# An attention and expert block on one core: which step of a gap takes a bank of the bursts, and goes first

## The reference

```
h = layernorm(x) * (1 + ca) + sa
x = x + ga * attention(h)          # 16 heads of 16, softmax over 1024 keys, projection
h = layernorm(x) * (1 + cb) + sb
x = x + gb * ffn(h)                # one base matrix, and the adapter of 8 that rebuilds h best
```

## Time and profile before

| | us |
|---|---|
| median of 3 runs | 1008.89 |
| the 3 runs | 1008.31, 1010.95, 1008.89 |
| span of the profiled execution, first to last instruction | 1004.2 |
| PE busy, share of the span | 962.7, 96% |
| DVE busy | 813.2, 81% |
| ACT busy | 661.7, 66% |
| granted TensorE clock, mean over the span | 0.988 |

### The profile page before, as it was taken

How to read it: one execution, slowest core, us unless ns; L and a number is a source line. 1 busy time by engine, 2 the same in 40 slices (tenths; PEclk the granted TensorE clock), 3 DMA queues, 4 the chain that set the end, 5 groups by cost and what they waited for, 6 DMA issues and landing times.

```text
span 1004.2 us, 16485 instructions
## 1 busy us (share of the span) xinstructions
PE 962.7 (96%) x5794; PEld 480.8 (48%) x5794; DVE 813.2 (81%) x1657; ACT 661.7 (66%) x1295; POOL 284.4 (28%) x391
## 2 busy tenths in 40 slices
PE   6989999999899999999999999999999999999998
PEld 5444344343344445554454454545454455644476
DVE  4789989899688887788888888788778788889455
ACT  2148787887577777667668786766657767666831
POOL 4210133022155241200336431300237413116320
PEclk9879999999899999999999999999999999999999
DMA  6850051242550513242223511404424311132001
GB/s 180 141 92 23 12 107 45 56 95 71 80 96 12 96 34 66 44 85 81 70 87 60 85 44 45 75 13 78 130 70 80 58 29 35 38 96 77 29 6 48
DMA packets 47890, 66.93 MB, mean 67 GB/s; under 512 B 12139, under 2 KB 32112, under 8 KB 47796
## 3 DMA queue, kind: packets, MB, share of 16 engines
q1 hardware_dynamic: 46572, 65.00, 29.9%
q0 software_dynamic: 384, 0.79, 0.5%
q10 hardware_dynamic: 852, 0.09, 0.1%
HBM read 27.48 MB, written 12.59 MB: 40 GB/s over the span
## 4 chain that ended last, share of the span: by engine, by line
PE 77%; DVE 9%; ACT 5%; issue 2%; POOL 2%; DMA 2%; SPq 1%; ACTq 0%; DVEq 0%; POOLq 0%
PE pE L811 25%; PE pO L811 22%; PE pX L811 18%; PE pM L811 11%; DVE mx L1293 4%; ACT P L1118 2%; DMA QO<-lo 1%; ACT h1T L1159 1%; DVE h2f L1454 1%; ACT h2f L1205 1%; ACT hi L1175 1%; DVE lo L1374 1%; SPq L1867 0%; DVE junk L1430 0%; DMA P<-in_wmod 0%
## 5 line engine op out<-in xcount | busy, mean ns | idle before, releaser
L1293 DVE TENSOR_REDUCE mx<-pM 128x1 f32<-128x512 f32 x1006 | 629.7, 682 | 76.7 <-PE pM L811 71.4
L1118 ACT ACTIVATE P<-pE 128x512 f32<-128x512 f32 x996 | 526.7, 601 | 181.1 <-PE pE L811 177.8
L811 PE MATMUL pM<-KO,QO 48*128 48x512 f32 x1006 | 370.7, 455 | 6.8 <-DMA QO<-lo 3.3
L811 PE MATMUL pE<-QO,KO 50*128 50x512 f32 x996 | 349.2, 438 | 11.9 <-ACT h1T L1159 5.1
L811 PEld LDWEIGHTS pE<-QO,KO 50*128 50x128 f32 x996 | 164.9, 187 | 234.1 <-issue 125.1
L811 PE MATMUL pO<-P,V 128*17 128x512 f32 x2048 | 257.9, 598 | 5.1 <-ACT P L1118 5.1
L811 PEld LDWEIGHTS pM<-KO,QO 48*128 48x128 f32 x1006 | 164.3, 187 | 41.3 <-DVE mx L1293 28.8
L811 PEld LDWEIGHTS pO<-P,V 128*17 128x17 f32 x2048 | 40.5, 96 | 103.2 <-issue 88.1
L1695 POOL CAST mh<-mxc 128x16 fp32r<-128x16 f32 x32 | 6.5, 203 | 285.7 <-DVE mxc L1302 285.5
L811 PE MATMUL pX<-h1T,wqkv_s 128*128 128x512 f32 x112 | 59.2, 642 | 1.9 <-DVE lo L1374 1.5
L1754 POOL TENSOR_TENSOR Hs<-h2f,Hs 128x512 fp32r<-128x512 f32 x28 | 35.7, 1284 | 83.6 <-ACT Hs L1235 68.3
(11 more groups left out here) (301 smaller groups left out, 1023.4 us busy)
## 6 DMA issues: line engine op xcount, KB each, us to landing
outs<-osb SPq DMA_DIRECT2D x31, 256.0 KB, 2.9
KO<-hi SPq DMA_DIRECT2D x56, 128.0 KB, 4.0
QO<-hi SPq DMA_DIRECT2D x56, 128.0 KB, 5.1
x<-in_x SPq DMA_DIRECT2D x20, 256.0 KB, 3.6
out<-x SPq DMA_DIRECT2D x16, 256.0 KB, 2.1
AT<-outs SPq DMA_DIRECT2D x15, 256.0 KB
asum<-wsum SPq DMA_DIRECT2D x15, 256.0 KB
KO<-lo SPq DMA_DIRECT2D x28, 128.0 KB, 3.6
```

The costliest lines, as they stand in the source:

```text
L811: return e.matmul(o, lhsT, rhs, start=start, stop=stop)
L1118: e.activation(P[:, u % 3, j, :], bank(s), ACT.Exp).then_inc(*empties(s))
L1293: e.tensor_reduce(mx[:, hq % 2, k:k + 1, kh], bank(s), AX.X, ALU.max, negate=True).then_inc(*empties(s))
```

## The change

A new function `arrange` goes over the finished list, gap by gap, between the first and the last E. In a gap it looks at the banked steps. One of them "stays": the one whose pieces are already open in the side bank, or else one left open by this gap, or else the last. The others are "ahead" if each is whole within the gap, is of another kind than the one that stays, and needs nothing of the same gap. Then their pieces go to the head of the gap, ahead of the copies, the quiet steps, P V and the step that stays, and they take a bank of the bursts (0 to 5). If one of them does not qualify, the gap is left alone. Nothing is added to or taken from the work.

```diff
--- before.py
+++ after.py
@@ -471,11 +471,41 @@
     return out
 
 
+def arrange(out):
+
+    first = next(n for n, s in enumerate(out) if s[0] == "E")
+    stop = max(n for n, s in enumerate(out) if s[0] == "E")
+    made, ahead, held, gap = list(out[:first]), set(), None, []
+    for s in out[first:stop + 1]:
+        if s[0] not in ("E", "M", "mmax"):
+            gap.append(s)
+            continue
+        if gap:
+            seen = [x if isinstance(x[0], tuple) else (x, 0) for x in gap]
+            here = list(dict.fromkeys(x for x, _ in seen if x[0] in BANKED))
+            ends = [x for x in here if (x, PIECES.get(x[0], 1) - 1) in seen]
+            open_ = [x for x in here if x not in ends]
+            stays = held or (open_ or here or [None])[-1]
+            front = [x for x in here if x != stays and x in ends and (x, 0) in seen and (not stays or x[0] != stays[0])
+                     and not any(d == y for d, _ in before(x) for y, _ in seen)]
+            if len(front) == len(here) - (stays in here):
+                ahead.update(front)
+                made += [y for y, x in zip(gap, seen) if x[0] in front]
+                made += [y for y, x in zip(gap, seen) if x[0] not in front]
+            else:
+                made += gap
+            held = open_[-1] if open_ else None if held in ends else held
+            gap = []
+        made.append(s)
+    return made + gap + list(out[stop + 1:]), ahead
+
+
 class Steps:
 
 
     def __init__(self):
-        self.list, self.nth, self.turn = order(), {}, {}
+        self.list, ahead = arrange(order())
+        self.nth, self.turn = {}, {}
         kinds, uses, at = Counter(), Counter(), {}
         begun, unfinished, burst = False, set(), -1
         for n, s in enumerate(self.list):
@@ -505,7 +535,9 @@
                 late = kinds["PV"] == NU
                 taken = {self.turn[x][0] for x in unfinished}
                 free = range(7)
-                if begun and not late:
+                if s in ahead:
+                    free = MB + EB
+                elif begun and not late:
                     free = ((5, 6) if not kinds["E"] or kinds["M"] == NM else
                             (XB,) if s[0] not in SHORT and at.get(XB, -1) < burst else
                             MB + EB if unfinished or at.get(XB, -1) > burst else MB + EB + (XB,))
```

## The result

The changed kernel takes 1015.0 us (median of 5, 1014.02 to 1015.84) against 1008.89 us (5 runs, 1005.70 to 1010.95): the ratio is 1.0075, with a 95% interval of 1.0058 to 1.0092, so it is slower by 6 to 9 us. The forecast was 1012.5 us with a range of 1005 to 1017: right in sign, and the time is inside the range, but the loss is twice the forecast 3.6 us.

A forecast was written before the change was run, and what follows sets the result against it. PE was taken to set the pace, busy 96% of the span, with DVE close behind. The terms summed as 10.8 - 15.7 + 5.5 + 2.4 + 0.6 = +3.6 us, taking the median from 1008.9 to 1012.5 us, range 1005 to 1017.

The forecast's parts named there:

- (a): Head of 47 changed gaps: PE waits for the exponential of the burst's first E, +10.8 us.
- (b): Bursts behind changed gaps: third E no longer stalls on the step that held its bank, -15.7 us at most.
- (c): Bursts behind the 21 bank swaps: third E newly stalls on the first step, such as gsq, +5.5 us.
- (d): Three gaps with qk's open piece last: DVE's lo delays the next maxima, 0.8 us each, +2.4 us.
- (e): Six freed stalls ahead of a lone P V, where DVE sets the period: 0.1 us each given back, +0.6 us.
- Level: Rival, chance 0.37: (c) and (d) half hidden because DVE comes sooner to head steps, -4.0, giving 1008.5 us.
- Faster: Rival, chance 0.17: third E's stalls return in full, (c) and (d) do not arise, -4.9, giving 1004.0 us.
- Rotation only: Rival, chance 0.05: ACT and DVE set the period, so (b) is all given back, +18.7, giving 1027.6 us.

The follow-up runs named there:

- Experiments 4: The changed kernel with the head step taking a maxima bank (0 to 2), freed later than the first E's: 1024.45 us, ratio 1.0167 to the kernel before.
- experiment 5: First E's exponential cut to 64 of 512 columns in the 46 bursts ahead of changed gaps: on the changed kernel 1005.76 us, on the kernel before 1005.43 us.
- e4: The change applied only in the 12 gaps that ended in ln1turn or xturn, against the kernel before: 1007.23 us, ratio 0.9971.
- e11: Kernel before, with the burst-bank step put between two side-bank pieces in 6 gaps and ln1turn or xturn moved to the head in 6 more: 1006.78 us, ratio 0.9980.
- e3: The change applied only in the 20 gaps that ended in a turn of the maxima or a select, against the kernel before: 1014.48 us, ratio 1.0032.

## Why the prediction came out as it did

**(a), the wait at the head: right, and the main term.** 0.24 us a gap was forecast and 12.8/46 = 0.28 read, of which the one gap where POOL was late is 1.3 us by itself. Experiments 4 and 5 change it in both directions and the time follows, by +7.2 and -9.9 us. The sentence that failed a little is the one that bounded it by ACT alone: a step moved ahead of P V also loses P V's cover for its own input.

**(b), the third E freed: right in size** (15.3 of 15.7 us), and e4 shows that it is real time. **(c), the front's hold on that bank: right** (5.2 of 5.5 us): the trace has the waits on gsq's reductions where they were put, at 424 and 662 us.

**(d): right in kind, counted in the wrong gaps.** Two of its three gaps cost 1.1 us each where 0.8 was taken; the third was counted against the diff's own rule; and three gaps in which a piece of half or enc is put last were left out, and cost 1.2 us. Together 3.4 us against 2.4.

**(e), given back: a little short.** It was put at 0.6 us, for six gaps ahead of a lone P V. The second bursts took 4.3 us, of them 3.4 for (d), so 0.9 is left for (e); and 0.8 us more, clock set aside, stand in bursts further on, which the sum did not have at all. My reading, which no run isolates: what was saved at the third E brought the next bursts forward, but not DVE, whose maxima and reductions are the same as before, and a later burst then waited for them.

**The size.** Forecast 3.6 us, measured 7.3 +- 0.7 at equal clock. Of the 3.7 us between them, by the trace, 1.0 is (d), 0.9 the starts and the changed gaps together, 1.1 is (e) and the bursts further on, and 0.1 (b) and (c); 0.6 is not placed, and within the noise. No single term failed: all erred to the same side. The time lay in the range all the same, since the range was 12 us wide and took in any loss up to 8 us.

**The rivals.** *Level* fell: DVE did not come sooner to the heavy heads. *Faster* had set its own deciding point, a head wait under 0.17 us; it was 0.28. With the wait cut, experiment 5 did come out on that side, by 1.4 +- 0.7 us. *Rotation only*, which the prediction tied to the rule of the Trainium skill (Perfetto Trace Analysis, Matmuls), was right about the head and not about the third E: its +18.7 us would have needed nothing to come back. The rule itself asks only that groups rotate through different banks; it does not speak of what a freed bank gives back.

The chances given, 0.46 to slower, were fair to the terms, which nearly cancel. But I let the bounds of the terms work both ways, where (d) and (e), counted in a few gaps only, had far more room to grow than to shrink.

## What to carry to other kernels

A bank just filled is a costly one to write next: before putting a step straight behind a burst, read when the first evacuation of that burst ends (here 0.2 to 0.3 us into the gap), and look for a place half a microsecond later that still has work behind it. Sort the places that a rule would change by what each has to win, and apply it only there: here, at equal clock, 12 places gained 2 us and the other 34 lost 10. And when an order changes, ask of every step in it, not only of the heaviest, whether its part on the engine that is nearly as busy now stands ahead of work it stood behind before, and follow the bursts for two or three rounds.

## What the runs showed that was not expected

The mean granted clock of a run lies between 0.981 and 0.990 for the kernel before and between 0.978 and 0.990 over all versions, and the time moves with it by more than small changes do: 0.65 us for each 0.001. Stretches at the lower level make it up. In e11's profiled execution, busy times and clock of such a stretch (window, PE, PEld, DVE, ACT, POOL, PEclk, DMA share, GB/s):

```profile
702.00:706.00 4.00, 4.00 (x20) 1.13 (x22) 2.32 (x5) 2.20 (x5) 1.45 (x2) 0.50 0.54 152
```

The timeline of PE in the same profile, from 700.41 us on (start, duration, line, operands):

```profile
700.41 0.49 PE L856 MATMUL pM<-KO,QO 48*128 48x512 f32 x1
...
702.33 1.91 PE L856 MATMUL pO<-P,V 128*17 128x512 f32 x8
704.16 0.79 PE L856 MATMUL pE<-QO,KO 50*128 50x512 f32 x1
```

The clock is 0.50 here, the 1.2 GHz level: eight matmuls of P V take 1.91 us in place of 1.05, and the next burst, up to a P V at 705.74, 1.58 us in place of 0.9. The level fell at 701.2 us. From 698.6 us up to there PE had gone through scores in which each M came 0.6 us behind the last, waiting for DVE, where an unhindered pair takes 0.29. That alone does not bring the clock down: the kernel before goes through the same scores at the same pace, waiting for DVE too, and its clock stays at 1.00 there; from its P V to the next burst it is 0.98 us, against 1.83 here. This is also why two spans of a few microseconds' difference are not yet a difference of the kernels, and why a burst-by-burst comparison of two profiles has to set the stretches at the lower level aside first: they are 1.5 us of what stood as "other bursts" between the two kernels, and nearly all of the 4.0 us in e3's.
